# One core, a fused three-block model: chunk 0 goes through turning and the input product while x still comes in, and GpSimd prepares the experts' weights beside the first layer's chunks

## The reference, cut to what matters

```python
h = x_tokens                 # mean over 128 outputs of x @ W.T + b: a weighted sum of 4 features
h = concat([h, txt], axis=1)                       # (64, 96, 64)
h = h + ssm(layernorm(h))                          # changed part
h = h + experts(layernorm(h))                      # 16 experts, top 2
h = h + attention(layernorm(h))
h = h + lstm(layernorm(h))                         # 96 steps in sequence

def ssm(x):
    h = x @ Win.T + bin_
    for l in range(4):                             # state-space layers, one after the other
        y_t  = state . mean(C_l) + u_t @ D_l.T
        state = A_l state + (u_t @ B_l.T)          # over 96 time steps
        h = layernorm(gelu(y) + h)
    return layernorm(h) @ Wout.T + bout
```

## Time and profile before

| what | value |
|---|---|
| time, median of 3 runs (lowest to highest) | 752.15 us (748.07 to 757.14) |
| the profiled execution's own time | 749.54 us |
| its span | 747.8 us |
| busy: PE, DVE, ACT, POOL | 682.9, 504.4, 371.0, 230.9 us |
| mean granted TensorE clock | 0.973 |

### The profile page before, as it was taken

How to read it: one execution, slowest core, us unless ns; L and a number is a source line. 1 busy time by engine, 2 the same in 40 slices (tenths; PEclk the granted TensorE clock), 3 DMA queues, 4 the chain that set the end, 5 groups by cost and what they waited for, 6 DMA issues and landing times.

```text
span 747.8 us, 17174 instructions
## 1 busy us (share of the span) xinstructions
PE 682.9 (91%) x6848; PEld 399.8 (53%) x6848; DVE 504.4 (67%) x1118; ACT 371.0 (50%) x721; POOL 230.9 (31%) x215
## 2 busy tenths in 40 slices
PE   5799999889999999888998999979799998999996
PEld 5677876562424223552343443357577776566553
DVE  3868999778565863854587667369777774465644
ACT  2334555425665546544454565536565655333332
POOL 4265899713424040311132102125323422000000
PEclk9999999959999999999999999989999999999999
DMA  9951000024223230001331322000000000000000
GB/s 185 176 81 27 2 3 2 1 72 169 91 99 120 100 119 16 3 30 70 101 100 57 101 85 76 7 1 2 2 2 2 1 2 2 13 11 9 13 11 13
DMA packets 42503, 36.94 MB, mean 49 GB/s; under 512 B 20936, under 2 KB 29944, under 8 KB 42424
## 3 DMA queue, kind: packets, MB, share of 16 engines
q1 hardware_dynamic: 41338, 35.60, 17.8%
q10 hardware_dynamic: 1088, 0.26, 0.2%
HBM read 33.85 MB, written 1.97 MB: 48 GB/s over the span
## 4 chain that ended last, share of the span: by engine, by line
PE 58%; DVE 22%; ACT 8%; issue 6%; DMA 2%; POOL 2%; SPq 1%; DVEq 0%; ACTq 0%; POOLq 0%
PE PS L1916 12%; PE PS L1903 11%; PE PS L1879 5%; PE PS L1951 3%; PE PS L1930 3%; PE PS L2007 2%; PE PS L2018 2%; PE PS L1972 2%; DVE am L1384 2%; PE PS L1865 2%; DVE LS L1474 2%; DVE LS L1487 2%; PE PS L1664 2%; ACT LS L995 1%; PE PS L1672 1%
## 5 line engine op out<-in xcount | busy, mean ns | idle before, releaser
L1916 PE MATMUL PS<-Y,W1f 64*128 64x512 f32 x384 | 110.7, 653 | 4.6 <-ACT XC L874 3.6
L1903 PE MATMUL PS<-XC,w2s 128*64 128x512 f32 x384 | 106.0, 632 | 0.4 <-ACT BIG L865 0.4
L874 ACT ACTIVATE XC<-PS 128x1024 f32<-128x1024 f32 x68 | 69.3, 1022 | 52.2 <-PE PS L1903 49.9
L1345 DVE TENSOR_TENSOR Y<-XD,UF 128x512 f32<-128x512 f32 x96 | 69.9, 733 | 6.1 <-DMA UF<-gd 3.2
L1879 PEld LDWEIGHTS PS<-LS,V 64*64 64x64 f32 x1140 | 40.6, 134 | 51.4 <-DVE LS L1487 47.5
L655 POOL TENSOR_TENSOR st<-st,mhalf 128x8 f32<-128x8 f32 x12 | 21.5, 1795 | 134.3 <-DVE st L1332 134.3
L1879 PE MATMUL PS<-LS,V 64*64 64x32 f32 x1140 | 51.1, 222 | 8.7 <-DVE LS L1487 6.4
L1903 PEld LDWEIGHTS PS<-XC,w2s 128*64 128x64 f32 x384 | 19.4, 137 | 73.6 <-issue 62.0
L1916 PEld LDWEIGHTS PS<-Y,W1f 64*128 64x128 f32 x384 | 30.7, 189 | 44.8 <-issue 27.8
L1474 DVE SCALAR_TENSOR_TENSOR LS<-LS 128x32 f32<-128x32 f32 x96 | 19.5, 203 | 49.7 <-ACT LS L989 26.6
L670 POOL TENSOR_TENSOR st<-st,mhalf 128x8 f32<-128x8 f32 x6 | 10.1, 1689 | 115.4 <-DVE st L1465 115.4
(11 more groups left out here) (255 smaller groups left out, 1455.8 us busy)
## 6 DMA issues: line engine op xcount, KB each, us to landing
...
```

The source lines that it names most:

```text
L874: act.activation(Hb[:, b:b + 2, :], PS[:, b:b + 2, :], ACT.Relu).then_inc(S("m_h"), 1)
L1345: dve.tensor_tensor(Rb[:, n % 4, :], XD[:, q * 512:(q + 1) * 512], GB[:, n % NS, :], ALU.mult).then_inc(S("m_x"), 1)
L1903: mm = pe.matmul(PS[64 * h:64 * h + 64, 6, :], w2s[:, 2 * p + h, :], Hb[:, n % 2 * 2 + h, :], start=(p == 0), stop=(p == E // 2 - 1))
L1916: mm = pe.matmul(PS[:, n % 2 * 2 + h, :], W1f[r, 2 * p + h, :], Rb[r, n % 4, :], start=True, stop=True)
```

## The change

It moves calls; no operation is added or taken away.

- SyncE: the eight DMAs of the layer weights are issued ahead of chunk 1 of x, and not ahead of chunk 2.
- TensorE, ACT and VectorE in the opening: chunk 0 goes through centring, turning and `win(0)`, and the layer weights are turned, while chunks 1 to 3 are still being folded. `feature_major(0)` stands ahead of the Toeplitz kernels.
- TensorE in the loop: `normalised(n+1)` instead of `normalised(n+2)`, and it stands between `du` and `spread`.
- VectorE in the loop: `front(3)` to `front(5)` and `back(3)` to `back(5)` are now inside steps 0 to 2, and `ssm_in(n+2)` is behind them, where `ssm_in(n+3)` was.
- ACT: `squares_0`, `ssm_x` and `ssm_uf` in step with this.
- GpSimd: two of W1f's eight slices behind each of the norms of steps 1 to 4, the gate weights and b3 behind step 5, and U3 and V3 behind the second chunk's preparation for the experts. Before, these stood one each behind steps 6 to 18.

```diff
--- before.py
+++ after.py
@@ -473,7 +473,7 @@
 
             xv = x.rearrange("b (m s) i f -> s b m (i f)", s=2)
             for c in XFOLD:
-                if c == 2:
+                if c == 1:
                     layer_weights()
                 for s in range(2):
                     sp.dma_start(Xr[64 * s:64 * s + 64, c * CH:(c + 1) * CH, :],
@@ -609,21 +609,20 @@
             ln_pool(pool, 0, lambda c: X[:, c * CH:(c + 1) * CH, :])
 
 
-            scaled = ((b3[:, :, :], 1.0 / D), (U3[:, 0:3:2, :], 0.5), (V3[:, 0:3:2, :], 0.25), (V3[:, 1, :], 0.5))
             W1P = E // 8
             for n in range(NS3):
                 ssm_scale(pool, n)
-                if n == NJ:
+                if n == 1:
+                    pool.wait_ge(S("ld_w1"), 16 * 6)
+                if n in (1, 2, 3, 4):
+                    for e0 in (2 * W1P * (n - 1), 2 * W1P * (n - 1) + W1P):
+                        e = slice(e0, e0 + W1P)
+                        seq(pool.tensor_tensor(W1f[:, e, :], W1f[:, e, :], W10[:, e, :], ALU.subtract), "w1c")
+                elif n == 5:
+                    seq(pool.tensor_tensor(GWs[:, :], GWs[:, :], gw0[:, :], ALU.subtract), "w1c")
                     pool.wait_ge(S("ld_at"), 16 * 8)
-                    pool.wait_ge(S("ld_ls"), 16 * 12)
-                    pool.wait_ge(S("ld_w1"), 16 * 6)
-                if NJ <= n < NJ + 4:
-                    seq(pool.tensor_scalar(scaled[n - NJ][0], scaled[n - NJ][0], scaled[n - NJ][1], None, ALU.mult), "wsc")
-                elif NJ + 4 <= n < NJ + 12:
-                    e = slice((n - NJ - 4) * W1P, (n - NJ - 3) * W1P)
-                    seq(pool.tensor_tensor(W1f[:, e, :], W1f[:, e, :], W10[:, e, :], ALU.subtract), "w1c")
-                elif n == NJ + 12:
-                    seq(pool.tensor_tensor(GWs[:, :], GWs[:, :], gw0[:, :], ALU.subtract), "w1c")
+                    seq(pool.tensor_scalar(b3[:, :, :], b3[:, :, :], 1.0 / D, None, ALU.mult), "wsc")
+
             def prepared(c):
                 sc = slice(c * CH, (c + 1) * CH)
                 pool.wait_ge(S("en_v"), c + 1)
@@ -642,6 +641,9 @@
 
             prepared(0)
             prepared(1)
+            pool.wait_ge(S("ld_ls"), 16 * 12)
+            for w, f in ((U3[:, 0:3:2, :], 0.5), (V3[:, 0:3:2, :], 0.25), (V3[:, 1, :], 0.5)):
+                seq(pool.tensor_scalar(w, w, f, None, ALU.mult), "wsc")
 
             def settle(j, part):
                 r = int(part[-1]) if part != "ga" else 0
@@ -771,37 +773,40 @@
             power(2)
             tokens(1)
             power(3)
-            tokens(2)
             squares_0(0)
             power(4)
-            tokens(3)
+            tokens(2)
             power(5)
+            ssm_x(0)
             squares_0(1)
             power(6)
-            ssm_x(0)
+            tokens(3)
+            ssm_uf(0)
             squares_0(2)
             ssm_x(1)
-            squares_0(3)
-            ssm_uf(0)
-            ssm_x(2)
-            squares_0(4)
             ssm_c(0)
             ssm_uf(1)
-            squares_0(5)
+            ssm_x(2)
             ssm_gelu(0)
-            ssm_x(3)
+            squares_0(3)
             ssm_c(1)
             ssm_uf(2)
-            ssm_x(4)
             for n in range(NS3):
+                if 3 <= n + 3 < NJ:
+                    ssm_x(n + 3)
                 if n + 1 < NS3:
                     ssm_gelu(n + 1)
-                ssm_uf(n + 3)
-                if n + 2 < NS3:
+                if 4 <= n + 4 < NC:
+                    squares_0(n + 4)
+                if n < 3:
+                    ssm_sq(n)
                     ssm_c(n + 2)
-                ssm_sq(n)
-                if n == 0:
-                    ssm_x(5)
+                    ssm_uf(n + 3)
+                else:
+                    ssm_uf(n + 3)
+                    if n + 2 < NS3:
+                        ssm_c(n + 2)
+                    ssm_sq(n)
             ssm_uf(NS3 + 3)
 
             def gates_exp(p):
@@ -1104,39 +1109,35 @@
 
 
             krylov(0)
-            for f in range(1, NF):
-                tokens(0, f)
+            tokens(0, 1)
+            tokens(0, 2)
             krylov(1)
-            for f in range(1, NF):
-                tokens(1, f)
+            tokens(0, 3)
+            front(0)
             krylov(2)
-            front(0)
+            tokens(1, 1)
+            back(0)
+            layer_weights()
+            krylov(3)
+            tokens(1, 2)
+            tokens(1, 3)
+            krylov(4)
+            front(1)
             tokens(2, 1)
             tokens(2, 2)
-            krylov(3)
+            krylov(5)
+            back(1)
+            dve.wait_ge(S("ld_bd"), 16 * 8)
+            ssm_in(0)
             tokens(2, 3)
-            back(0)
-            front(1)
-            krylov(4)
-            for f in range(1, NF):
-                tokens(3, f)
-            krylov(5)
-            layer_weights()
-            dve.wait_ge(S("ld_bd"), 16 * 8)
-            back(1)
+            krylov(6)
             front(2)
-            krylov(6)
+            tokens(3, 1)
+            kernels()
             back(2)
-            front(3)
-            kernels()
-            ssm_in(0)
-            back(3)
-            front(4)
             ssm_in(1)
-            back(4)
-            front(5)
-            ssm_in(2)
-            back(5)
+            tokens(3, 2)
+            tokens(3, 3)
 
             def ssm_y(n):
                 j = n % NJ
@@ -1166,12 +1167,18 @@
                                   ALU.mult, ALU.add).then_inc(S("s_v"), 1)
 
             for n in range(NS3):
+                if n == 0:
+                    front(3)
                 ssm_y(n)
                 if n:
                     ssm_var(n - 1)
                 ssm_centre(n)
                 if n < 3:
-                    ssm_in(n + 3)
+                    back(n + 3)
+                if n + 2 < NJ:
+                    ssm_in(n + 2)
+                if n < 2:
+                    front(n + 4)
             ssm_var(NS3 - 1)
 
             def ssm_out(j):
@@ -1594,10 +1601,11 @@
                     last = pe.matmul(PS[:, 3, l * T:l * T + T], BB[:, l, :, :].rearrange("p a b -> p (a b)"), Gk[:, l, :], start=True, stop=True)
                 last.then_inc(S("p_w"), 1)
 
-            for i in range(5):
+            for i in range(3):
                 powers(i)
             weights_turn()
-            powers(5)
+            powers(3)
+            powers(4)
 
             xk = halves(X)
             def normalised(j):
@@ -1698,25 +1706,28 @@
             pe.wait_ge(S("ii"), 2)
             pe.wait_ge(S("one"), 1)
             normalised(0)
+            powers(5)
+            win(0)
             powers(6)
-            win(0)
+            feature_major(0)
             kernels()
             normalised(1)
-            for n in range(NS3 + NJ):
-                if 1 <= n <= NS3:
+            win(1)
+            for n in range(1, NS3 + NJ):
+                if n <= NS3:
                     toeplitz(n - 1)
                 if n == NS3 + 4:
                     projections()
                 feature_major(n)
-                if 1 <= n <= NS3:
+                if n <= NS3:
                     du(n - 1)
+                    if n + 1 < NJ:
+                        normalised(n + 1)
                     spread(n - 1)
-                elif n:
+                    if n + 1 < NJ:
+                        win(n + 1)
+                else:
                     out_product(n - 1 - NS3)
-                if n + 2 < NJ:
-                    normalised(n + 2)
-                if n + 1 < NJ:
-                    win(n + 1)
 
 
             held = {4: (("s_uf", NS3 + 5),), 5: (("s_uf", NS3 + 6),)}
```

## The result

The changed kernel takes 771.85 us (median of 4 runs, 764.76 to 776.21) beside 754.64 for the kernel before (4 runs on the same chip): ratio 1.0254, 95% interval 1.0187 to 1.032. It is slower. The forecast was 762 with a range to 771, so the direction was right, and the time is just outside the range. The profiled execution took 775.77 us, 26.2 us more in its span than that of before.

The account below looks back on a forecast made before the run. The chain was over half TensorE, a fifth VectorE. Start -4.2, first layer +14.1, clock +5, lag -0.8, later steps -2.6 gave +11.5, or +10 without double counting; on the 752.15 median, 762 us, range 752 to 771.

Parts of the forecast that it names:

- The start: Opening up to step 0's Gelu: first bias sum near 31 us, Gelu at 44.5 for 48.66, a gain of 4.2.
- The first layer: Steps 0 to 5: steps no longer overlap, 37.0 us against 22.9, a loss of 14.1 us.
- The circle: First-layer loop: VectorE's late bias sum and GpSimd's norm behind `back` hold TensorE, whose spread the next Gelu awaits; steps to 9.4 us.
- The clock: TensorE in the first layer: idle time lowers the granted clock, 3.1 us at half per loop, 5 us lost in all.
- The later steps: Steps 5 to 23: GpSimd's slices leave steps 10 to 17, 59.6 us becomes 57.0, a gain of 2.6 (0 to 4.2).
- C: Rival, first layer: TensorE's clock stays down until step 5, +18.6, 771 us; chance 0.11.
- E: Rival, opening: the loop does not form, earlier start and recovered slices remain, -8.2, 744 us; chance 0.06.
- D: Rival, gate product near 148 us: the half-clock stretch is missed, saving about 5 us, with B 752 us; chance 0.08.

Follow-up runs that it names:

- the filler: Changed kernel with nine unread dummy matmuls on TensorE ahead of each turning of chunks 2 to 5; 765.45 us, ratio 1.0226 to the kernel before.
- the list alone: Kernel before with the changed kernel's order of GpSimd's weight slices and scalings; 757.68 us, ratio 1.0111 to the kernel before.
- the front alone: Changed kernel with GpSimd's weight slices and scalings back where they stood before; 774.72 us, ratio 1.0353 to the kernel before.

## Why the prediction was right and where it failed

**The start** was right: 30.42 against "near 31", the first Gelu at 43.38, inside 43 to 46, 1.1 us before the value taken. That is 5.3 us gained against 4.2. The measured value is one of two: in the eleven profiled executions with the moved front the Gelu of step 0 came at 43.2 to 43.8 (six) or at 45.6 to 46.5 us (five), and in the late ones the `du` and spread ahead of it still took 1.97 and 1.9 to 2.0 us in place of 1.1 to 1.2 and 1.08. The prediction had both ends, 43 at the fast rates and 46 at the slow ones.

**The first layer** had the right mechanism. The circle was forecast with its order of waits, and the runs showed both of its holds, the bias sum and the norm behind `back`: with the bias sum alone moved it stayed, with both moved it opened. Its size: 37.0 us forecast and 38.96 with the clock kept up, so the chain of durations was 2.0 short, mostly in step 2 (10.75 for 9.4), which the filler did not keep at full clock throughout.

**The clock** was under-sized: 5 us, of which 1.4 was taken back as counted twice, against 6.8 that the filler gave back. TensorE's waits for the bias sum were 2.47, 3.49, 3.80 and 1.51 us, near the forecast 2 to 4, but I took the half-clock stretch of each loop as short as the shortest row had it, 3.1 us. In windows of half a microsecond they are 6.8, 6.8, 6.8 and 10.2 us, and the last one ends at 91.7, in step 5. The first layer and its clock together gave +22.9 where the sum had 14.1 + 3.6.

**The later steps** are the step that failed. The prediction said "The 59.6 us can shrink to 18 x 3.08" and took 57.0, a gain of 2.6 with 0 as its worst. It was a loss of 7.0, so the term was off by 9.6 us of the 13.7 by which the sum (+10.1) fell short of the +23.8. The rest is the first layer with its clock, 5.2 too low, less the start, which gained 1.1 more than forecast. What the runs showed in place of the gain: 4.7 us from the locked steps, and 2.3 us in steps 5 to 8, mostly a clock still at its lower level in step 5, where the prediction let the clock's cost end. The 3.08 us, called TensorE's own pace, stands in no row; undisturbed steps of before took 3.02 to 3.1. Two things were wrong in the working. First, I read the 5.1 us above an even pace as what slices cost VectorE. The trace of before says otherwise, on GpSimd, between two powers:

```profile
114.70 1.64 POOL L178 TENSOR_TENSOR st<-st,mhalf 128x8 f32<-128x8 f32 x1
116.42 1.06 POOL L180 TENSOR_TENSOR UT<-XC,st 128x512 f32<-128x512 f32 x1
117.44 0.72 POOL L624 TENSOR_TENSOR W1f<-W1f,EX 128x256 f32<-128x256 f32 x1
118.24 1.64 POOL L178 TENSOR_TENSOR st<-st,mhalf 128x8 f32<-128x8 f32 x1
```

Power, product and slice come round in 3.54 us, and the sums of steps 16 to 21 there are 3.53 apart: with a slice GpSimd itself is the pace. Second, I asked what leaves those steps and not in what state GpSimd enters them. The norms and the first slices it did make up for, while the steps were long; its powers of steps 3 and 4 in the changed kernel still waited for VectorE:

```profile
87.71 1.64 POOL L178 TENSOR_TENSOR st<-st,mhalf 128x8 f32<-128x8 f32 x1 [3.58 <-DVE st L1166]
...
93.84 1.64 POOL L178 TENSOR_TENSOR st<-st,mhalf 128x8 f32<-128x8 f32 x1 [1.44 <-DVE st L1166]
```

The last four slices, the gate weights and b3 (90.43 to 102.54 us) then stand beside steps 5 to 8, just when the steps get short, and leave it two steps behind. In the steady part it has hardly any slack to catch up in: 1.64 + 1.04 and the gaps against a step of 3.1, and less when its product waits out a two-input operation. So it no longer waits for VectorE's variance, and nothing holds its product off the centring. I cited the shared port for a gain of the slices' full 0.72 us, and did not turn the same rule on the 24 products of 1.04 us that stay beside VectorE's two-input operations. The experiments bear out the pattern as the cause: it came with the list alone, was absent with the front alone, and was gone wherever the product was held behind `ssm_y(n+3)`. Why it sets in at step 9 in the changed kernel and at 18 in most others was seen, not settled. Being behind is not enough: GpSimd is two steps behind from step 6 on in those others too, but there its products of steps 7 to 14 start 0.6 us or more behind the centring, mostly beside the sum, which then isn't held up, and in the changed kernel 0.03 us behind the centring. The locked onset at 9 was seen only with both the slow first layer and the new list.

**The rivals.** C, the clock down until step 5, gave 771 and lies nearest to the time, but that is luck: of the 45.77 us the clock had some 6.8, not 13.5, and what made up the number is the loss in the later steps, which C had as a gain. E did not occur, nor did D: the gate product shifted with the rest, by 24.2 us. It was to hang on an idle time of TensorE under 1.76 us, but the product waited 1.76 us in both kernels; before, the clock fell during the wait (L1748 takes 3.56 us), in the changed kernel only 1.1 us into the product (L1759 takes 2.55).

**Sum on the median.** The terms as measured give +23.8 in the profiled executions, the medians differ by 17.2. Before was profiled 5.1 us under its median, the changed kernel 3.9 us over its own. That an arrival time in the opening passes on to the end was roughly true of one profile (615.3 us behind `ssm_y(23)` before, 617.7 in the changed kernel), but the fifteen profiles spread over 12 us there.
